# Adapter A placed beside W1's columns, W's product made three chunks ahead, the next x turned two chunks earlier: a two-layer kernel on one Trainium2 core

## The chip, the cores and the metric

The kernel runs on one core of a Trainium2 chip. The metric is the device time of one execution in microseconds, lower being better.

## The reference

For each of 8 batch entries, x is [256, 1024] and mask is [1024, 1024] of 0 and 1. Two residual layers follow one another:

```python
# first layer: W and b shared, one coefficient and one mask for each batch entry
y = x + einsum('bsi,oi->bso', x, W0) + b0 + coeff[b] * einsum('bsi,bio->bso', x, 2 * mask - 1)
# second layer: W1 and b1 shared, a rank-16 adapter chosen by itok_B_6_15 for each entry
A, Bw = lora_A_w[ids], lora_B_w[ids]
out = y + einsum('bsd,od->bso', y, W1) + b1 + einsum('bsr,bor->bso', einsum('bsd,brd->bsr', y, A), Bw)
```

The mask of each entry makes a weight matrix of its own: W0 + I + coeff * (2 * mask - 1), with 4 MB of int32 mask read for each.

## The kernel before

**Precision.** Every float32 operand of a product is split into two fp32r parts, hi and lo, and a product is made of three: hi with hi, hi with lo, lo with hi.

**Chunks.** The work is 64 chunks, n = 8 * b + c: batch entry b (called a batch below), and 128 of the 1024 columns of y (c). For chunk n:

- SyncE (`load_mask`, L166) loads 512 KB of mask into one of four slots of `wm`, once the chunk four before has left it (semaphore `w_lo`).
- VectorE `make_w` (L482) makes 2 * coeff * mask + W0 in place; ScalarE `chunk_hi` (L343) makes `whi`; VectorE `chunk_lo` (L491) makes `wlo`. `whi` and `wlo` have three slots (WS = 3).
- TensorE `layer1` (L614): for each of 8 blocks k, one matmul of 512 columns (`whi` by x hi and x lo side by side) and one of 256 (`wlo` by x hi), into PSUM bank 4 or 5.
- ScalarE `half_y` (L370), VectorE `make_y` (L499), ScalarE `y_parts_hi` (L379) and VectorE `y_parts_lo` (L504) turn the bank into `yhl`, y hi and y lo, in one of two slots.
- TensorE, one chunk later (m = n - 1): `adapter_h` (L632), one matmul of 512 columns with the adapter's A as weights, summed over the batch's 8 chunks in bank 6; and `layer2` (L640), for each half of the rows (st) and of the output columns (oh) three matmuls of 512 columns with y as weights and W1 moving, into banks 0 to 3.

**End of a batch.** After the eighth chunk, `h_parts_hi` (three ScalarE copies, L385) and `h_parts_lo` split the adapter's h into the rows of `ht`. `finish` (L657) adds h times adapter B and the bias b1 to the four banks, one matmul of 512 columns each; three of them stand before the last three matmuls of `layer2`. ScalarE and VectorE copy two banks each into `zst` (`move_z`), and SyncE stores them.

**Order.** Each engine runs its list in the order written. SyncE's list for program step n is: load the mask of chunk n + 4; and, where c = 0, wait for the four moves of the batch before, store the four pieces, and issue the six small copies of adapter B into `bt` (`load_bt`, L201). So the masks of chunks 8b + 5 and later stand behind the stores of batch b - 1 in SyncE's queue. At c = 2 it loads the next x (`load_x`, four transfers of 256 KB). VectorE's list for step n in batches 1 to 7 is:

```python
if n + 2 < NS:
    make_w(n + 2)
if c in (5, 7) and b + 1 < NB:
    rows_lo(b + 1, (c - 5) // 2)
if n + 2 < NS:
    chunk_lo(n + 2)
make_y(n)
if c == 0:
    h_parts_lo(b - 1)
y_parts_lo(n)
```

and after it, at c = 0, two moves, and at c = 4 and 6 `turn_rows` (L462), a 32x32 block transpose of half of the next x, whose split (`rows_hi`, `rows_lo`) follows at c = 5 and 7. Batch 0 also transposes W0, W1, A and B on TensorE (`turn_unit`).

## Time and profile before

| | us |
|---|---|
| median of 3 runs | 433.26 (432.2 to 433.63) |
| the profiled execution, its own time | 435.75 |
| its span, first to last instruction | 434.1 |
| TensorE matmul busy (2049 matmuls) | 409.7 |
| VectorE busy | 287.1 |
| ScalarE busy | 184.6 |
| GpSimd busy | 24.0 |

The mean granted clock of TensorE over the span is 0.978 of full speed. The chain that ended last is made of TensorE work for 88% of the span and of VectorE work for 6%. Durations of matmuls in the trace include their latency, so the distance from one start to the next tells what one costs.

### The profile page before, as it was taken

How to read it: one execution, taken by the hardware profiler on the slowest of the kernel's cores; microseconds unless marked ns; L12 is line 12 of the kernel's file. 1: busy time of each engine (PE TensorE's matmuls, PEld its weight loads, DVE VectorE, ACT ScalarE, POOL GpSimd, SP SyncE). 2: the span in 40 equal slices, each digit the busy share in tenths (PEclk: the TensorE clock that was granted, in tenths of full speed). 3: DMA queues.
4: the chain of work that ended last, by engine and by line, in shares of the span. 5: the costliest groups of instructions: out<-in, count | busy, mean ns of one | idle time of the engine just before them, and what ended most of it. 6: DMA issues, size and time to landing. Idle time of an engine off the chain costs nothing.

```text
span 434.1 us, 5456 instructions
## 1 busy us (share of the span) xinstructions
PE 409.7 (94%) x2049; PEld 342.3 (79%) x2049; DVE 287.1 (66%) x336; ACT 184.6 (43%) x288; POOL 24.0 (6%) x47
## 2 busy tenths in 40 slices
PE   3579998978999999999999999999999999999996
PEld 3568886757888888888888888888888888888884
DVE  0475658676688666776588767776678667866512
ACT  2264555454334533363343434444245433453312
POOL 4325401000000000000000000000000000000000
PEclk9788999899999999999999999999999999999999
DMA  6996796416943399309931595319921894237002
GB/s 224 253 333 195 207 211 179 86 48 151 249 125 94 108 193 222 97 1 233 237 100 50 131 240 150 98 74 209 236 64 36 196 241 120 61 110 169 2 0 97
DMA packets 90845, 63.28 MB, mean 146 GB/s; under 512 B 3515, under 2 KB 84419, under 8 KB 90820
## 3 DMA queue, kind: packets, MB, share of 16 engines
q1 hardware_dynamic: 89588, 59.28, 55.3%
q0 software_dynamic: 1232, 3.67, 2.7%
q8 instruction: 16, 0.26, 0.3%
q14 instruction: 9, 0.07, 0.1%
HBM read 51.39 MB, written 8.39 MB: 138 GB/s over the span
## 4 chain that ended last, share of the span: by engine, by line
PE 88%; DVE 6%; ACT 2%; DMA 2%; issue 1%; SPq 1%; ACTq 0%; DVEq 0%
PE ps L625 27%; PE ps L627 13%; PE ps L652 13%; PE ps L651 13%; PE ps L653 13%; PE ps L635 3%; PE ps L611 3%; PE ps L663 2%; DMA cs<-in_condB_coeff_dram 2%; DVE wm L488 1%; DVE wlo L495 1%; ACT whi L350 1%; DVE w1lo L460 1%; DVE xhl L471 1%; DVE xt L465 0%
## 5 line engine op out<-in xcount | busy, mean ns | idle before, releaser
L625 PE MATMUL ps<-xhl,whi 128*128 128x512 f32 x512 | 187.8, 405 | 2.0 <-DVE wlo L495 1.2
L627 PE MATMUL ps<-xhl,wlo 128*128 128x256 f32 x512 | 145.1, 283 | 0.0
L495 DVE SCALAR_TENSOR_TENSOR wlo<-wm,cs_minus,whi 128x1024 fp32r<-128x1024 f32 x64 | 83.0, 1296 | 53.2 <-ACT whi L350 52.8
L625 PEld LDWEIGHTS ps<-xhl,whi 128*128 128x128 f32 x512 | 97.7, 191 | 25.1 <-DVE wlo L495 1.5
L350 ACT ACTIVATE whi<-wm,cs_minus 128x1024 fp32r<-128x1024 f32 x64 | 73.7, 1151 | 81.7 <-DVE wm L488 80.5
L651 PE MATMUL ps<-w1hi,yhl 128*128 128x512 f32 x256 | 102.0, 398 | 0.0
L652 PE MATMUL ps<-w1lo,yhl 128*128 128x512 f32 x256 | 100.7, 394 | 0.0
L653 PE MATMUL ps<-w1hi,yhl 128*128 128x512 f32 x256 | 100.5, 393 | 0.0
L627 PEld LDWEIGHTS ps<-xhl,wlo 128*128 128x128 f32 x512 | 98.1, 192 | 2.5
L488 DVE SCALAR_TENSOR_TENSOR wm<-wm,cs_twice,w0t 128x1024 f32<-128x1024 int32 x64 | 81.8, 1278 | 11.7 <-ACT w0t L331 11.5
L652 PEld LDWEIGHTS ps<-w1lo,yhl 128*128 128x128 f32 x256 | 48.5, 189 | 10.7
L653 PEld LDWEIGHTS ps<-w1hi,yhl 128*128 128x128 f32 x256 | 48.2, 188 | 10.8
L651 PEld LDWEIGHTS ps<-w1hi,yhl 128*128 128x128 f32 x256 | 48.6, 190 | 7.9
L376 ACT ACTIVATE ysum<-ps,b0col 128x256 f32<-128x256 f32 x64 | 30.0, 469 | 41.2 <-PE ps L627 40.6
L383 ACT ACTIVATE yhl<-ysum 128x256 fp32r<-128x256 f32 x64 | 26.7, 417 | 44.1 <-DVE ysum L502 43.5
L506 DVE TENSOR_TENSOR yhl<-ysum,yhl 128x256 fp32r<-128x256 f32 x64 | 27.1, 424 | 24.0 <-ACT yhl L383 23.7
L502 DVE TENSOR_TENSOR ysum<-ps,ysum 128x256 f32<-128x256 f32 x64 | 26.8, 419 | 19.2 <-ACT ysum L376 19.2
L465 DVE STREAM_TRANSPOSE xt<-xraw 128x1024 f32<-128x1024 f32 x14 | 30.4, 2174 | 0.0
L361 ACT ACTIVATE xhl<-xt 128x1024 fp32r<-128x1024 f32 x14 | 14.9, 1062 | 31.1 <-DVE xt L465 31.1
L635 PE MATMUL ps<-yhl,at 128*128 128x512 f32 x64 | 25.9, 404 | 0.0
L460 DVE TENSOR_TENSOR w1lo<-ps,w1hi 128x512 fp32r<-128x512 f32 x16 | 10.9, 688 | 13.6 <-ACT w1hi L341 13.6
L331 ACT ACTIVATE w0t<-ps 128x512 f32<-128x512 f32 x16 | 9.5, 597 | 22.8 <-PE ps L611 22.8
(50 smaller groups left out, 178.7 us busy)
## 6 DMA issues: line engine op xcount, KB each, us to landing
wm<-in_mask_Bx4096x_ik_dram SPq DMA_DIRECT2D x64, 512.0 KB, 5.8
out_dram<-zst SPq DMA_DIRECT2D x32, 256.0 KB, 2.5
xraw<-in_x_dram SPq DMA_DIRECT2D x28, 256.0 KB, 7.4
w1raw<-_L_cond_base_weight_dram SPq DMA_DIRECT2D x8, 512.0 KB, 6.5
bt<-bhl SPq DMA_DIRECT2D x48, 64.0 KB, 2.9
w0raw<-in_L_cond_W_dram POOLq DMA_DIRECT2D x5, 512.0 KB, 6.7
w0raw<-in_L_cond_W_dram SPq DMA_DIRECT2D x3, 512.0 KB, 9.2
xrows<-in_x_dram SPq DMA_DIRECT2D x2, 512.0 KB, 7.0
```

Source lines behind the costliest of these rows:

```text
L350: nc.scalar.activation(whi[:, n % WS, :, :], wm[:, n % MS, :].rearrange("p (k o) -> p k o", k=KT), ACT.Identity, bias=cs_minus[:, b:b + 1] ...
L376: nc.scalar.activation(ysum[:, n % 2, :], ps[:, L1B + n % 2, S:2 * S], ACT.Identity, bias=b0col[:, n % KT:n % KT + 1]).then_inc(y_half, 1)
L465: nc.vector.transpose(xt[:, :, :].rearrange("p t (n q) -> p n t q", q=Q), xraw[:, :, :].rearrange("p n (i k) -> p n k i", k=KT)[:, :, g * ...
L488: nc.vector.scalar_tensor_tensor(chunk, chunk.bitcast(I32), cs_twice[:, b:b + 1], w0t[:, c, :, :].rearrange("p k o -> p (k o)"), ALU.mult, ...
L495: nc.vector.scalar_tensor_tensor(wlo[:, s, :, :], wm[:, n % MS, :].rearrange("p (k o) -> p k o", k=KT), cs_minus[:, b:b + 1], whi[:, s, :, ...
L506: nc.vector.tensor_tensor(yhl[:, n % 2, S:2 * S], ysum[:, n % 2, :], yhl[:, n % 2, 0:S].bitcast(F32), ALU.subtract).then_inc(y_lo, 1)
L625: nc.tensor.matmul(ps[:, bank, :], whi[:, s, k, :], xhl[:, b % 2, k, :], start=(k == 0), stop=False, skip_group_check=True)
L627: op = nc.tensor.matmul(ps[:, bank, 0:S], wlo[:, s, k, :], xhl[:, b % 2, k, 0:S], start=False, stop=(k == KT - 1), skip_group_check=True)
L635: op = nc.tensor.matmul(ps[:, HB, :], at[:, c, b * 2 * R:b * 2 * R + P], yhl[:, n % 2, :], start=(c == 0), stop=(c == KT - 1))
L651: nc.tensor.matmul(ps[:, Z0 + j, :], hi, w1hi[:, c, cols], start=(c == 0), stop=False)
L652: nc.tensor.matmul(ps[:, Z0 + j, :], hi, w1lo[:, c, cols], start=False, stop=False)
L653: op = nc.tensor.matmul(ps[:, Z0 + j, :], lo, w1hi[:, c, cols], start=False, stop=False)
```

## The change

- `w1hi` and `w1lo` get 16 free columns on either side of W1's 1024. From batch 1 on GpSimd copies the batch's adapter A (hi and lo) into them (`place_a`): left of W1 for even batches, right of it for odd ones. `adapter_h` stays for batch 0 alone. From batch 1 on `layer2` covers the 1040 columns of A and W1 in three groups of 352, 344 and 344 columns for each half of the rows, so 18 matmuls a chunk in place of 13, into banks 0, 2, 3 and 1, 6, 7.
- h now comes out with the rows of x on the partitions. At the batch's end ScalarE copies it out (`move_h`), TensorE turns it back with two transposes into a free bank (`turn_h`), and the split into `ht` takes two ScalarE copies instead of three. For this the groups with A (j = 0) of the last chunk are multiplied one program step earlier, ahead of the next batch's first `layer1`.
- All six `finish` matmuls stand at the end, one behind another. There are six moves and six stores (328 to 352 columns) in place of four of 512.
- VectorE's list for step n becomes `chunk_lo(n + 2)`, `make_w(n + 3)`, then `rows_lo` (c = 3 and 5), `make_y(n)`, ..., with `turn_rows` at c = 2 and 4. ScalarE makes `chunk_hi(n + 3)` after `y_parts_hi(n)`. The number of slots of `wm`, `whi` and `wlo` is unchanged, and so is SyncE's order of masks, stores and `load_bt`. `load_x(b + 2)` stands at c = 7 instead of `load_x(b + 1)` at c = 2.
- A memset of the adapter's padding goes away in batch 0.

```diff
+
+    WR = R + D + R
+    EDGES = (0, 352, 696, D + R)
+    ZB = ((0, 2, 3), (1, 6, 7))
+
...
+
+    def z_cut(b, j):
+
+
+        g = j if b % 2 == 0 else 2 - j
+        lo, hi = EDGES[g], EDGES[g + 1]
+        if b % 2 == 0:
+            skip = R if j == 0 else 0
+            return slice(lo, hi), slice(skip, hi - lo), slice(lo + skip - R, hi - R), slice(0, R)
+        end = hi - R if j == 0 else hi
+        return slice(R + lo, R + hi), slice(0, end - lo), slice(lo, end), slice(hi - lo - R, hi - lo)
...
         w0t = sb("w0t", [P, KT, KT, P])
-        w1hi = sb("w1hi", [P, KT, D], F32R)
-        w1lo = sb("w1lo", [P, KT, D], F32R)
+        w1hi = sb("w1hi", [P, KT, WR], F32R)
+        w1lo = sb("w1lo", [P, KT, WR], F32R)
...
-        zst = sb("zst", [P, 4, HALF])
+        zst = sb("zst", [P, ST, D])
...
-        at = sb("at", [P, KT, (NB + 3) * 2 * R], F32R)
+        at = sb("at", [P, KT, 2 * P], F32R)
+        h_row = sb("h_row", [P, ST, R])
...
-            def store_z(b, st, oh):
-                if oh == 0:
-                    sp.wait_ge(z_moved_act, 2 * b + st + 1)
+            def store_z(b, q):
+                st = q // 2 if b == 0 else q // 3
+                if q % 2 == 0:
+                    sp.wait_ge(z_moved_act, moves_before(b) + q // 2 + 1)
                 else:
-                    sp.wait_ge(z_moved_dve, 2 * b + st + 1)
-                j = 2 * st + oh
-                dst = out[b, st * P:(st + 1) * P, oh * HALF:(oh + 1) * HALF]
-                sp.dma_start(dst, zst[:, j, :]).then_inc(z_stored[j], 16)
+                    sp.wait_ge(z_moved_dve, moves_before(b) + q // 2 + 1)
+                cols = slice(q % 2 * HALF, (q % 2 + 1) * HALF) if b == 0 else z_cut(b, q % 3)[2]
+                sp.dma_start(out[b, st * P:(st + 1) * P, cols], zst[:, st, cols]).then_inc(z_stored[st], 16)
...
@@ -243,17 +280,17 @@
                 if n == 7:
                     load_bt(0)
                 if c == 0 and b > 0:
-                    for st in range(ST):
-                        for oh in range(2):
-                            store_z(b - 1, st, oh)
+                    for q in range(4 if b == 1 else 6):
+                        store_z(b - 1, q)
                     load_bt(b)
-                if c == 2 and b + 1 < NB:
-                    load_x(b + 1)
+                if n == 2:
+                    load_x(1)
+                if c == 7 and b + 2 < NB:
+                    load_x(b + 2)
+            for q in range(6):
+                store_z(NB - 1, q)
             for st in range(ST):
-                for oh in range(2):
-                    store_z(NB - 1, st, oh)
-            for j in range(4):
-                sp.wait_ge(z_stored[j], 16 * NB)
+                sp.wait_ge(z_stored[st], 16 * stores_before(NB))
...
+            def place_a(b):
+                if b == 1:
+                    pool.wait_ge(parts_lo, parted(number["a", 0, 1]))
+                elif b >= 3:
+                    pool.wait_ge(l2_done, KT * (b - 1))
+                slot = 0 if b % 2 == 0 else R + D
+                for part, row in enumerate((w1hi, w1lo)):
+                    nc.gpsimd.tensor_copy(row[:, :, slot:slot + R],
+                                          at[:, :, (2 * b + part) * R:(2 * b + part + 1) * R].bitcast(F32)).then_inc(a_placed, 1)
...
-            nc.gpsimd.memset(at[:, :, 2 * P:].bitcast(F32), 0.0).then_inc(consts_set, 1)
...
+            place_a(1)
+            place_a(2)
+            pool.wait_ge(z_done, sums_before(1))
+            nc.gpsimd.memset(ht[0:80, :].bitcast(F32), 0.0).then_inc(h_cleared, 1)
+            for b in range(3, NB):
+                place_a(b)
...
-                nc.scalar.activation(zst[:, 2 * st, :], ps[:, Z0 + 2 * st, :], ACT.Copy).then_inc(z_moved_act, 1)
+            def move_h(b):
+                act.wait_ge(h_done, b + 1)
+                if b >= 2:
+                    act.wait_ge(h_turned, b - 1)
+                cut = z_cut(b, 0)[3]
+                nc.scalar.activation(h_row[:, :, :], ps[:, ZB[0][0]:ZB[1][0] + 1, cut],
+                                     ACT.Copy).then_inc(h_moved, 1)
+
+            def h_parts_hi(b):
+                act.wait_ge(h_turned, b)
+                act.wait_ge(h_cleared, 1)
+                act.wait_ge(z_done, sums_before(b))
+                nc.scalar.activation(ht[0:R, :], ps[0:R, L1B + (KT * b + 9) % 2, 0:S], ACT.Copy).then_inc(h_hi, 1)
+                act.wait_ge(h_hi, h_hi_before(b) + 1)
+                nc.scalar.activation(ht[96:96 + R, :], ht[0:R, :].bitcast(F32), ACT.Copy).then_inc(h_hi, 1)
...
+
+            def move_z(b, q):
+                st, j = divmod(q, 3)
+                act.wait_ge(z_done, sums_before(b) + q + 1)
+                act.wait_ge(z_stored[st], 16 * stores_before(b))
+                _, cut, cols, _ = z_cut(b, j)
+                nc.scalar.activation(zst[:, st, cols], ps[:, ZB[st][j], cut], ACT.Copy).then_inc(z_moved_act, 1)
 
             copy_w0(0, 0)
             copy_w0(0, 1)
@@ -433,22 +504,30 @@
                 if n == 1:
                     act.wait_ge(b1_in, 16)
                     nc.scalar.activation(b1hi[:, :], b1raw[:, :], ACT.Copy).then_inc(bias_hi, 1)
+            chunk_hi(KT + 2)
             for n in range(KT, NS):
                 b, c = divmod(n, KT)
-                if c in (5, 7) and b + 1 < NB:
-                    rows_hi(b + 1, (c - 5) // 2)
-                if n + 2 < NS:
-                    chunk_hi(n + 2)
+                if c in (3, 5) and b + 1 < NB:
+                    rows_hi(b + 1, (c - 3) // 2)
                 half_y(n)
-                if c == 0:
+                if c == 0 and b == 1:
+                    first_h_parts_hi()
+                elif c == 0:
                     h_parts_hi(b - 1)
                 y_parts_hi(n)
-                if c == 0:
-                    move_z(b - 1, 0)
-                    move_z(b - 1, 1)
+                if n + 3 < NS:
+                    chunk_hi(n + 3)
+                if c == 0 and b == 1:
+                    first_move_z(0)
+                    first_move_z(1)
+                elif c == 0:
+                    for q in (0, 2, 4):
+                        move_z(b - 1, q)
+                if c == 7:
+                    move_h(b)
             h_parts_hi(NB - 1)
-            move_z(NB - 1, 0)
-            move_z(NB - 1, 1)
+            for q in (0, 2, 4):
...
-                nc.vector.tensor_copy(zst[:, 2 * st + 1, :], ps[:, Z0 + 2 * st + 1, :]).then_inc(z_moved_dve, 1)
+            def h_parts_lo(b):
+                dve.wait_ge(h_hi, h_hi_before(b) + 1)
+                nc.vector.tensor_tensor(ht[32:32 + R, :], ps[0:R, L1B + (KT * b + 9) % 2, 0:S], ht[0:R, :].bitcast(F32),
+                                        ALU.subtract).then_inc(h_lo, 1)
...
+
+            def move_z(b, q):
+                st, j = divmod(q, 3)
+                dve.wait_ge(z_done, sums_before(b) + q + 1)
+                dve.wait_ge(z_stored[st], 16 * stores_before(b))
+                _, cut, cols, _ = z_cut(b, j)
+                nc.vector.tensor_copy(zst[:, st, cols], ps[:, ZB[st][j], cut]).then_inc(z_moved_dve, 1)
 
             dve.wait_ge(coeff_in, 16)
             nc.vector.tensor_scalar(cs_twice[:, :], cs[:, :], 2.0, None, ALU.mult).then_inc(coeff_made, 1)
@@ -555,26 +644,32 @@
                     dve.wait_ge(bias_hi, 1)
                     nc.vector.tensor_tensor(b1lo[:, :], b1raw[:, :], b1hi[:, :].bitcast(F32),
                                             ALU.subtract).then_inc(bias_lo, 1)
+            make_w(KT + 2)
             for n in range(KT, NS):
                 b, c = divmod(n, KT)
                 if n + 2 < NS:
-                    make_w(n + 2)
-                if c in (5, 7) and b + 1 < NB:
-                    rows_lo(b + 1, (c - 5) // 2)
-                if n + 2 < NS:
                     chunk_lo(n + 2)
+                if n + 3 < NS:
+                    make_w(n + 3)
+                if c in (3, 5) and b + 1 < NB:
+                    rows_lo(b + 1, (c - 3) // 2)
                 make_y(n)
-                if c == 0:
+                if c == 0 and b == 1:
+                    first_h_parts_lo()
+                elif c == 0:
                     h_parts_lo(b - 1)
                 y_parts_lo(n)
-                if c == 0:
-                    move_z(b - 1, 0)
-                    move_z(b - 1, 1)
-                if c in (4, 6) and b + 1 < NB:
-                    turn_rows(b + 1, (c - 4) // 2)
+                if c == 0 and b == 1:
+                    first_move_z(0)
+                    first_move_z(1)
+                elif c == 0:
+                    for q in (1, 3, 5):
+                        move_z(b - 1, q)
+                if c in (2, 4) and b + 1 < NB:
+                    turn_rows(b + 1, (c - 2) // 2)
             h_parts_lo(NB - 1)
-            move_z(NB - 1, 0)
-            move_z(NB - 1, 1)
+            for q in (1, 3, 5):
+                move_z(NB - 1, q)
 
         @block.tensor
...
-            def finish(b, st, oh):
+            def layer2(n, st, j):
+                b, c = divmod(n, KT)
+                q = 3 * st + j
+                if c == 0 and q == 0:
+                    pe.wait_ge(a_placed, 2 * b)
+                if c == 0 and b == 1 and q == 0:
+                    pe.wait_ge(z_moved_act, 2)
+                    pe.wait_ge(z_moved_dve, 2)
+                elif c == 0 and b > 1 and q % 2 == 0:
+                    pe.wait_ge(z_moved_act, moves_before(b - 1) + q // 2 + 1)
+                elif c == 0 and b > 1:
+                    pe.wait_ge(z_moved_dve, moves_before(b - 1) + q // 2 + 1)
+                cols = z_cut(b, j)[0]
+                dst = ps[:, ZB[st][j], 0:cols.stop - cols.start]
+                hi = yhl[:, n % 2, st * P:(st + 1) * P]
+                lo = yhl[:, n % 2, S + st * P:S + (st + 1) * P]
+                nc.tensor.matmul(dst, hi, w1hi[:, c, cols], start=(c == 0), stop=False, skip_group_check=True)
+                nc.tensor.matmul(dst, hi, w1lo[:, c, cols], start=False, stop=False, skip_group_check=True)
+                op = nc.tensor.matmul(dst, lo, w1hi[:, c, cols], start=False, stop=(c == KT - 1), skip_group_check=True)
+                if q == 5:
+                    op.then_inc(l2_done, 1)
+                if c == KT - 1 and q == 3:
+                    op.then_inc(h_done, 1)
+
+            def turn_h(b):
+                pe.wait_ge(h_moved, b)
+                for st in range(ST):
+                    op = nc.tensor.transpose(ps[0:R, L1B + (KT * b + 9) % 2, st * P:(st + 1) * P], h_row[:, st, :], ident[:, :])
+                op.then_inc(h_turned, 1)
+
...
+
+            def finish(b, st, j):
+                if st == 0 and j == 0:
+                    pe.wait_ge(h_hi, h_hi_before(b + 1))
+                    pe.wait_ge(h_lo, b + 1)
+                    pe.wait_ge(bt_in, 96 * (b + 1))
+                _, cut, cols, _ = z_cut(b, j)
+                nc.tensor.matmul(ps[:, ZB[st][j], cut], ht[:, st * P:(st + 1) * P], bt[:, cols],
+                                 start=False, stop=True, skip_group_check=True).then_inc(z_done, 1)
 
...
+                    pe.wait_ge(consts_set, 2)
                     pe.wait_ge(w0_copied, copied(number["w0", 2, 1]))
                 if m < KT:
                     pe.wait_ge(parts_lo, parted(number["w1", m, 1]))
-                adapter_h(m)
-                layer2(m, 0, 0)
-                if 0 < n < KT:
-                    turn_unit("w1", n, 0)
-                layer2(m, 0, 1)
-                layer2(m, 1, 0)
-                if 0 < n < KT:
-                    turn_unit("w1", n, 1)
-                if m % KT == KT - 1:
-                    finish(m // KT, 0, 0)
-                    finish(m // KT, 0, 1)
-                    finish(m // KT, 1, 0)
-                layer2(m, 1, 1)
-                if m % KT == KT - 1:
-                    finish(m // KT, 1, 1)
-
+                if m < KT:
+                    adapter_h(m)
+                    first_layer2(m, 0, 0)
+                    if n < KT:
+                        turn_unit("w1", n, 0)
+                    first_layer2(m, 0, 1)
+                    first_layer2(m, 1, 0)
+                    if n < KT:
+                        turn_unit("w1", n, 1)
+                    if m == KT - 1:
+                        first_finish(0, 0)
+                        first_finish(0, 1)
+                        first_finish(1, 0)
+                    first_layer2(m, 1, 1)
+                    if m == KT - 1:
+                        first_finish(1, 1)
+                    continue
+                pe.wait_ge(y_lo, m + 1)
+                if m % KT < KT - 1:
+                    for st in range(ST):
+                        for j in range(3):
+                            layer2(m, st, j)
+                else:
+                    if n < NS:
+                        turn_h(m // KT)
+                    layer2(m, 0, 1)
+                    layer2(m, 1, 1)
+                    if n == NS:
+                        turn_h(m // KT)
+                    layer2(m, 0, 2)
+                    layer2(m, 1, 2)
+                    for st in range(ST):
+                        for j in range(3):
+                            finish(m // KT, st, j)
+                if n < NS and n % KT == KT - 1:
+                    pe.wait_ge(y_lo, n + 1)
+                    layer2(n, 0, 0)
```

## Rows read from the trace of the kernel before

**Rows 1.** The page: its head, and group rows of ScalarE and of the stores.

```profile
span 434.1 us, 5456 instructions
...
L350 ACT ACTIVATE whi<-wm,cs_minus 128x1024 fp32r<-128x1024 f32 x64 | 73.7, 1151 | 81.7 <-DVE wm L488 80.5
```

**Rows 2.** Busy time by stretch: batch 2, from its first sum to the next (PEclk 1.00 is full speed).

```profile
146.50:194.00 47.50, 47.50 (x238) 39.76 (x238) 34.38 (x40) 20.27 (x31) 0.00 (x0) 1.00 0.62 142
```

**Rows 3.** The chain that ended last: start, us; four transposes, and adapter_h two chunks apart.

```profile
37.14 0.44 PE ps L611 x4
...
151.07 0.24 PE ps L635
...
162.68 0.24 PE ps L635
```

**Rows 4.** Timeline, TensorE: adapter_h and the next layer-1 chunk (start, us, ...).

```profile
204.19 0.40 PE L635 MATMUL ps<-yhl,at 128*128 128x512 f32 x1
...
207.19 0.39 PE L625 MATMUL ps<-xhl,whi 128*128 128x512 f32 x1
```

**Rows 5.** Timeline, the last chunk: layer 1's end to both halves of y.

```profile
423.19 0.39 PE L635 MATMUL ps<-yhl,at 128*128 128x512 f32 x1
423.39 0.47 ACT L376 ACTIVATE ysum<-ps,b0col 128x256 f32<-128x256 f32 x1 [4.44 <-PE ps L627]
...
423.89 0.42 DVE L502 TENSOR_TENSOR ysum<-ps,ysum 128x256 f32<-128x256 f32 x1 [4.49 <-ACT ysum L376]
...
424.35 0.42 ACT L383 ACTIVATE yhl<-ysum 128x256 fp32r<-128x256 f32 x1 [0.49 <-DVE ysum L502]
...
424.80 0.43 DVE L506 TENSOR_TENSOR yhl<-ysum,yhl 128x256 fp32r<-128x256 f32 x1 [0.48 <-ACT yhl L383]
```

**Rows 6.** Timeline, VectorE alone, around a turn of x.

```profile
217.41 0.42 DVE L506 TENSOR_TENSOR yhl<-ysum,yhl 128x256 fp32r<-128x256 f32 x1 [0.48 <-ACT yhl L383]
217.75 2.19 DVE L465 STREAM_TRANSPOSE xt<-xraw 128x1024 f32<-128x1024 f32 x1
219.85 1.26 DVE L488 SCALAR_TENSOR_TENSOR wm<-wm,cs_twice,w0t 128x1024 f32<-128x1024 int32 x1
221.07 1.23 DVE L471 TENSOR_TENSOR xhl<-xt,xhl 128x1024 fp32r<-128x1024 f32 x1
```

**Rows 7.** Timeline, all engines, the end of batch 2 (SPq is SyncE's queue).

```profile
191.55 0.39 PE L635 MATMUL ps<-yhl,at 128*128 128x512 f32 x1
...
193.91 0.93 PE L663 MATMUL ps<-bt,ht 128*128 128x512 f32 x3
194.42 1.09 ACT L400 ACTIVATE zst<-ps 128x512 f32<-128x512 f32 x2 [0.60 <-PE ps L663]
...
195.04 1.83 SPq L218 DMA_DIRECT2D out_dram<-zst  x4
...
196.92 3.13 SPq L208 DMA_DIRECT2D bt<-bhl  x5
...
200.73 1.34 SPq L173 DMA_DIRECT2D wm<-in_mask_Bx4096x_ik_dram  x2
```

**Rows 8.** Time from issue to landing: all masks; the mask issued at 200.73; at 153.22.

```profile
DMA to landing us min/median/max: 3.8/5.8/12.6
...
wm<-in_mask_Bx4096x_ik_dram SPq DMA_DIRECT2D x1, 512.0 KB, 4.4
...
wm<-in_mask_Bx4096x_ik_dram SPq DMA_DIRECT2D x1, 512.0 KB, 5.5
```

**Rows 9.** Timeline, the end of batch 0: VectorE and the first sum.

```profile
98.39 0.41 DVE L511 TENSOR_TENSOR ht<-ps,ht 32x256 fp32r<-32x256 f32 x1
...
98.91 0.93 PE L663 MATMUL ps<-bt,ht 128*128 128x512 f32 x3 [1.78 <-ACT ht L394]
```

**Rows 10.** Timeline, the end of the last batch.

```profile
428.43 0.84 PE L663 MATMUL ps<-bt,ht 128*128 128x512 f32 x3
...
429.48 1.81 SPq L218 DMA_DIRECT2D out_dram<-zst  x4
```

More of the change, by code:

```diff
@@ L55, in x_split, with sums_before, moves_before, stores_before @@
         return 4 + 2 * (b - 1) + g + 1
+    def z_cut(b, j):
[6 more added lines that the diff above has]
+        return slice(R + lo, R + hi), slice(0, end - lo), slice(lo, end), slice(hi - lo - R, hi - lo)
+    def sums_before(b):
+        return 4 + 6 * (b - 1) if b else 0
+    def moves_before(b):
+        return 2 + 3 * (b - 1) if b else 0
+    def stores_before(b):
+        return 2 + 3 * (b - 1) if b else 0
+    def h_hi_before(b):
+        return 3 + 2 * (b - 1) if b else 0
     with ExitStack() as ctx:
@@ L116, in two_layer_kernel @@
         bt_in = sem("bt_in")
-        z_stored = [sem(f"z_stored{j}") for j in range(4)]
+        z_stored = [sem(f"z_stored{st}") for st in range(ST)]
         ident_set = sem("ident_set")
@@ L142, in two_layer_kernel @@
         l2_done = sem("l2_done")
+        a_placed = sem("a_placed")
         h_done = sem("h_done")
+        h_cleared = sem("h_cleared")
+        h_moved = sem("h_moved")
+        h_turned = sem("h_turned")
         h_hi = sem("h_hi")
@@ L156, in part_views @@
             if kind == "w1":
-                return (w1hi, w1lo)[part][:, c, h * HALF:(h + 1) * HALF], src
+                return (w1hi, w1lo)[part][:, c, R + h * HALF:R + (h + 1) * HALF], src
             if kind == "a":
-                dst = at[:, 4 * h:4 * h + 4, 0:2 * P].rearrange("p k (b two r) -> p k b two r", b=NB, two=2)
+                dst = at[:, 4 * h:4 * h + 4, :].rearrange("p k (b two r) -> p k b two r", b=NB, two=2)
                 return dst[:, :, :, part, :], src.rearrange("p (k b r) -> p k b r", k=4, b=NB)
@@ L383, in y_parts_hi, with first_h_parts_hi @@
                 nc.scalar.activation(yhl[:, n % 2, 0:S], ysum[:, n % 2, :], ACT.Copy).then_inc(y_hi, 1)
-            def h_parts_hi(b):
-                act.wait_ge(h_done, b + 1)
-                if b == 0:
-                    act.wait_ge(consts_set, 3)
-                else:
-                    act.wait_ge(z_done, 4 * b)
+            def first_h_parts_hi():
+                act.wait_ge(h_done, 1)
+                act.wait_ge(consts_set, 2)
                 nc.scalar.activation(ht[0:2 * R, :], ps[0:2 * R, HB, 0:S], ACT.Copy).then_inc(h_hi, 1)
@@ L638, in adapter_h, with first_layer2 @@
                     op.then_inc(h_done, 1)
-            def layer2(n, st, oh):
-                b, c = divmod(n, KT)
+            def first_layer2(c, st, oh):
                 j = 2 * st + oh
-                if c == 0 and b > 0:
-                    if oh == 0:
-                        pe.wait_ge(z_moved_act, 2 * (b - 1) + st + 1)
-                    else:
-                        pe.wait_ge(z_moved_dve, 2 * (b - 1) + st + 1)
-                hi = yhl[:, n % 2, st * P:(st + 1) * P]
-                lo = yhl[:, n % 2, S + st * P:S + (st + 1) * P]
-                cols = slice(oh * HALF, (oh + 1) * HALF)
+                hi = yhl[:, c % 2, st * P:(st + 1) * P]
+                lo = yhl[:, c % 2, S + st * P:S + (st + 1) * P]
+                cols = slice(R + oh * HALF, R + (oh + 1) * HALF)
                 nc.tensor.matmul(ps[:, Z0 + j, :], hi, w1hi[:, c, cols], start=(c == 0), stop=False)
```

32 lines of the change are left out of this document (16 added, 16 removed).

## The prediction

> **What bounds the kernel now.** I read the page first, for the span [rows 1]. The busy time by stretch then shows that a middle batch lasts 47.50 us and TensorE works in all of it at full clock [rows 2]; the other middle batches read alike. In the chain two adapter matmuls two chunks apart stand 11.61 us apart, so a chunk costs 5.80 us [rows 3]. Eight chunks are 46.42; the four finishing matmuls at 0.23 make 0.92; 0.17 is left, a short stall at the batch's end. So from batch 1 on the kernel is a queue of matmuls, and a chunk can only become shorter if TensorE has less to do and everything else still arrives in time. Batch 0 is ruled by transposes, splits and loads; the change hardly touches it except at its end.
>
> **What a matmul costs.** Layer 2 with the adapter is 13 matmuls of 512 columns in 3.00 us, and 2.99 on average (5.80 less layer 1) [rows 4]: 0.230 each. At 2.4 GHz 512 columns are 0.213, so some 0.016 comes on top. Layer 1 gets the other 2.81: eight pairs of 512 and 256 columns, 0.351 a pair against 0.320 for the columns, again 0.016 each. The width 344 isn't in the trace; it lies between 256 (0.122) and 512 (0.230), and by the same line it is 0.159, and 352 is 0.163. The new layer 2 is 6240 columns in 18 matmuls: 2.60 + 18 x 0.016 = 2.89, that is 0.10 less for a chunk, and a chunk costs 5.70. The bounds: no extra cost for the five more matmuls gives 0.18 less, an extra cost of 0.022 each gives nothing.
>
> The Trainium skill, TensorE: Matmul & The Clock Gate, section Back-to-back issue gap, gives a fixed 2.5 ns beside the columns. By that figure the new layer 2 would save 0.16 us a chunk, or 9.0 in all in place of 5.6; the trace disagrees, since 512 columns would then be 0.216 apart and are 0.230 [rows 4].
>
> **The sum on TensorE.** Layer 2: 56 chunks x 0.10 = 5.6 saved. Two transposes a batch, at 0.11 each [rows 3]: 7 x 0.22 = 1.5 added. Six finishing matmuls over the same columns in place of four: 7 x 0.03 = 0.2 added. The stall of 0.17 at six batch ends, if the new path of h is in time: 1.0 saved. Is it? Call T0 the end of layer 1 of a batch's first chunk. The transposes end near T0 + 0.45, ScalarE is then past half_y (T0 + 0.67 by the distances of [rows 5]), two copies of about 0.4 end at 1.5 and VectorE's part at about 1.55; the finish isn't wanted before 12 matmuls later, T0 + 2.1. Yes, with 0.5 to spare, so these edits are hidden. The GpSimd copies of A and the missing memset stand beside other work and are counted at nothing; uncovered, a copy would be some 1 us once a batch, but its columns aren't wanted for most of a batch.
>
> **The end of batch 0.** There VectorE is late and TensorE waits for h: h_parts_lo runs at 98.39 and the first finish at 98.91 after 1.78 idle [rows 9]. The new list puts make_w(11), 1.22 long [rows 6], ahead of make_y(8) and of this h. 1.2 us added.
>
> **The masks, where the gain goes.** make_w(n + 3) now stands in front of make_y(n) in VectorE's queue, but the mask loads are no earlier. The mask of chunk 8b + 5 is issued behind the stores and bt: at 200.73 where T0 is 191.55, so T0 + 9.2 [rows 7]. Before, it was used only in step 8b + 3. Now it is wanted in step 8b + 2, right after chunk_lo(8b + 4), near T0 + 10, which in itself puts it 4 us short. It is also issued later still: ScalarE does y_parts_hi (to 1.8), then chunk_hi of 1.15 [rows 1], and only then the first move, of about 0.5 (half of 1.09 for 512 columns is the upper bound [rows 7]); the stores start at T0 + 3.35. Six of them at 0.45 are 2.7, bt and what follows 3.8 (196.92 to 200.73): issue at T0 + 9.9. It lands 4.4 later, in one batch 5.5 [rows 8]; I take 4.5, so T0 + 14.4.
>
> Behind this make_w wait, in order on VectorE: make_y(8b + 2), y_parts_lo, turn_rows (new at c = 2), chunk_lo, make_w, rows_lo (new at c = 3), make_y(8b + 3), y_parts_lo. In starts from the landing: 0.06 wake, 1.22 make_w, 0.46 + 0.45 for y [rows 5], 0.34 to the turn, 2.10 turn, 1.22 make_w's like for chunk_lo, 1.22 make_w, 1.23 rows_lo [rows 6], 0.46 + 0.45 + 0.43 for y: 9.64, so T0 + 24.0. TensorE wants y of chunk 8b + 3 after layer 1 of 8b + 4. That is T0 + 5.90 (0.22 transposes, 1.92 for twelve matmuls, 0.95 finishing, 2.81 layer 1) + 3 x 5.70 = T0 + 23.0. It stands for 1.0 us. The y of 8b + 2 is just in time (T0 + 17.0 for 17.3). The second turn and split, at c = 4 and 5, let VectorE catch up nothing, as two steps take it 11.3 against 11.4 on TensorE, and it has caught up by c = 7 but for about 0.1. Batch 7 turns no x, so its lateness stays under the slack; batch 1 still has the four wide stores behind its sums and issues its mask some 2.8 after its second layer 1 (the others 4.0), and has none. So five batches, 2 to 6: 5 x 1.0 = 5.0 added.
>
> **The end.** Before, three finishing matmuls stand ahead of the last three of layer 2, and from 428.43 it is 5.6 to the end [rows 10]. Now all six stand behind: 0.7 later, a stall of 0.15 for h (its path is 1.33, six matmuls and two transposes between cover 1.17), and six stores at 0.45 in place of four, 0.7. Together 1.6 added.
>
> **Sum.** -5.6 + 1.5 + 0.2 - 1.0 + 1.2 + 5.0 + 1.6 = +2.9 on a span of 434.1. The profiled execution took 435.75 with what lies around its span; the median of the runs is 433.26, and the difference is added to that: 436.2.
>
> **Rivals.**
>
> *No lateness.* If the mask lands by T0 + 13.4, or VectorE's chain is 1 us shorter, TensorE never waits and the sum is -2.1: 431.2, faster. That is the other side, and its point is sharp: 1.0 us in a chain of 24. For it: landings vary, the shortest of the 64 takes 3.8 [rows 8], and x is no longer loaded right behind. Against it: three of the terms are exact distances of the trace, and the issue behind the stores can't be avoided. Chance 0.18.
>
> The Trainium skill, DMA: Bandwidth & Descriptors, section Anatomy of one DMA, fits 2.0 us plus bytes over 436 GB/s (measured for GpSimd's queue), an estimate of 3.2 us for 512 KB. By it the mask lands at T0 + 13.1 and this rival holds, 431.2; the trace has 4.4 and 5.5 for these transfers [rows 8], so it adds nothing to the chance.
>
> *Later masks.* At 5.5 to landing [rows 8] in every batch, y of 8b + 2 is late as well and each of five batches stands 2.1: 436.2 + 5.5 = 441.7. One batch of five shows it. Chance 0.12.
>
> *Something between:* landings at 4.0, or half of the batches, 432 to 434.5. Chance 0.17.
>
> *Narrow matmuls dearer:* if the fixed part is 0.022 or more at 344 columns, the 5.6 are gone. But then TensorE's steps are longer and VectorE's lateness shrinks by as much until c = 3, so only part shows: about 438. Chance 0.05.
>
> *The path of h late* by 0.5 at each batch end, for instance through the move queue on ScalarE: 7 x 0.5 = 3.5, 439.5. Against it the 0.5 to spare. Chance 0.05.
>
> The forecast: 0.43, with a range of its own of 434.7 to 438.
>
> **Range and chances.** A no-change would be within 0.3% (432.0 to 434.6), about what a measurement of this kernel can tell. The case without lateness, 431.2, is held at the low end and the case of later masks is cut at its upper part: 430.9 to 439.4. Faster: 0.18 and little else, 0.20. Same: the case between and the low tail of the forecast, 0.19. Slower: 0.61.
>
> **What the profile after would show.** Right: layer 2 as 18 matmuls 0.159 apart; make_w(8b + 5) idle in front for some 4 us, released by the mask's landing; TensorE idle about 1 us in front of layer 2 of chunk 8b + 3, released by VectorE's y_parts_lo, in batches 2 to 6; batches of 47.8; the first finish of batch 0 near 100.1. Wrong: middle batches of 46.8 with TensorE busy throughout (no lateness), or steps of 5.80 as before (narrow matmuls dearer), or waits in front of the finish. What would make it wrong most easily is the 1.0, a small difference between two sums of over 20 us.

## The result and the profile after

The changed kernel takes 439.88 us (439.2 to 441.95, 4 runs), the kernel before 433.44 in the same comparison: 1.46% slower, ratio 1.0146 (95% interval 1.0082 to 1.0209). The forecast was 436.2 with a range to 439.4: the direction is right, the size is more than twice what was forecast, and the time is outside the range. A second comparison, on another chip, gave 440.38 against 433.78, ratio 1.0135 (1.0102 to 1.0169).

The profiled execution of after spans 437.4, which looks like the forecast (434.1 + 2.9 = 437.0), but the two profiled executions are not alike in their granted clock: 0.978 before, 0.988 after. An execution of the changed kernel at 0.976 spans 439.0. That pair, +4.9, is the one to explain.

The page of after: the head, and the group of make_w (busy, mean ns of one, then idle before it and what ended most of that).

```profile
span 437.4 us, 6140 instructions
...
L567 DVE SCALAR_TENSOR_TENSOR wm<-wm,cs_twice,w0t 128x1024 f32<-128x1024 int32 x64 | 82.9, 1295 | 42.2 <-DMA wm<-in_mask_Bx4096x_ik_dram 32.0
```

VectorE waited for a mask for 32.0 us in all, where before there was one such wait of 0.25. The chain that ended last shows what that does; here it is in batch 3 (start, duration, engine and line).

```profile
196.99 0.79 PE ps L791 x5
197.78 0.93 DVE zst L607 x2
...
198.84 0.46 SPq L255
...
200.82 0.59 SPq L245
...
203.99 0.59 SPq L246
...
204.62 4.17 DMA wm<-in_mask_Bx4096x_ik_dram
208.82 1.28 DVE wm L567
210.10 0.34 DVE ysum L581
210.47 0.43 ACT yhl L436
...
211.26 2.24 DVE xt L544
213.50 1.17 DVE wlo L574
214.67 1.19 DVE wm L567
215.86 1.14 DVE xhl L550
217.00 0.34 DVE ysum L581
217.37 0.42 ACT yhl L436
217.81 0.44 DVE yhl L585
...
218.29 0.42 PE ps L762
```

It is a ring: the sums (L791), the moves, six stores (L255), six bt copies (L245, L246), the mask, then VectorE's list in its new order, and only then layer 2 on TensorE. Before, the chain stayed on TensorE through such a batch. TensorE's own timeline at both ends of the ring, with T0 = 194.72 at the transposes of h (L773):

```profile
194.72 0.38 PE L773 MATMUL ps<-ident,h_row 128*16 128x128 f32 x2
194.86 0.40 PE L762 MATMUL ps<-w1hi,yhl 128*128 128x344 f32 x1
195.10 0.32 PE L763 MATMUL ps<-w1lo,yhl 128*128 128x344 f32 x1
195.26 0.32 PE L764 MATMUL ps<-w1hi,yhl 128*128 128x344 f32 x1
...
218.29 0.42 PE L762 MATMUL ps<-w1hi,yhl 128*128 128x344 f32 x1 [0.64 <-DVE yhl L585]
```

The mask is issued at T0 + 9.9 and landed by T0 + 14.07 (208.79); y of chunk 8b + 3 is there at T0 + 23.5 (218.25). The matmuls of layer 2 stand 0.157 us apart at 344 columns and 0.161 at 352. The idle time printed is short of the whole stall, since it counts from the modelled end of the matmul before, not from where the next could have started.

### The profile page after: what moved, and what is told of

It is laid out like the page before. It is cut to its first block, busy times and chain, and to the rows that moved or that the text cites. A ratio compares the mean times of both kernels' runs of the same rounds, so it can differ in the third digit from the quotient of the medians.

```text
span 437.4 us, 6140 instructions
## 1 busy us (share of the span) xinstructions
PE 405.3 (93%) x2357; PEld 367.5 (84%) x2357; DVE 285.5 (65%) x343; ACT 177.1 (40%) x295; POOL 28.9 (7%) x61
## 4 chain that ended last, share of the span: by engine, by line
PE 62%; DVE 17%; SPq 7%; DMA 7%; ACT 3%; issue 2%; DVEq 0%; ACTq 0%
PE ps L720 18%; PE ps L762 9%; PE ps L764 9%; PE ps L722 9%; PE ps L763 9%; DMA wm<-in_mask_Bx4096x_ik_dram 5%; DVE wm L567 5%; SPq L245 3%; PE ps L706 3%; DVE xt L544 3%; DVE wlo L574 3%; SPq L255 3%; DVE xhl L550 2%; DMA cs<-in_condB_coeff_dram 2%; PE ps L791 1%
## 5 line engine op out<-in xcount | busy, mean ns | idle before, releaser
L762 PE MATMUL ps<-w1hi,yhl 128*128 128x344 f32 (+1 forms) x336 | 109.5, 326 | 5.4 <-DVE yhl L585 5.3
L567 DVE SCALAR_TENSOR_TENSOR wm<-wm,cs_twice,w0t 128x1024 f32<-128x1024 int32 x64 | 82.9, 1295 | 42.2 <-DMA wm<-in_mask_Bx4096x_ik_dram 32.0
L764 PE MATMUL ps<-w1hi,yhl 128*128 128x344 f32 (+1 forms) x336 | 107.7, 321 | 0.0
L763 PE MATMUL ps<-w1lo,yhl 128*128 128x344 f32 (+1 forms) x336 | 107.6, 320 | 0.0
L574 DVE SCALAR_TENSOR_TENSOR wlo<-wm,cs_minus,whi 128x1024 fp32r<-128x1024 f32 x64 | 81.9, 1280 | 23.7 <-ACT whi L403 23.7
L762 PEld LDWEIGHTS ps<-w1hi,yhl 128*128 128x128 f32 x336 | 63.1, 188 | 10.8 <-DVE yhl L585 8.5
L763 PEld LDWEIGHTS ps<-w1lo,yhl 128*128 128x128 f32 x336 | 63.2, 188 | 0.0
L764 PEld LDWEIGHTS ps<-w1hi,yhl 128*128 128x128 f32 x336 | 63.1, 188 | 0.0
L414 ACT ACTIVATE xhl<-xt 128x1024 fp32r<-128x1024 f32 x14 | 14.8, 1060 | 19.1 <-DVE xt L544 19.1
L706 PE MATMUL ps<-ident,w0raw 128*128 128x128 f32 x64 | 11.3, 312 | 7.2 <-POOL w0raw L301 5.3
```

The lines of the kernel that those rows point to most:

```text
L567: nc.vector.scalar_tensor_tensor(chunk, chunk.bitcast(I32), cs_twice[:, b:b + 1], w0t[:, c, :, :].rearrange("p k o -> p (k o)"), ALU.mult, ...
L574: nc.vector.scalar_tensor_tensor(wlo[:, s, :, :], wm[:, n % MS, :].rearrange("p (k o) -> p k o", k=KT), cs_minus[:, b:b + 1], whi[:, s, :, ...
L762: nc.tensor.matmul(dst, hi, w1hi[:, c, cols], start=(c == 0), stop=False, skip_group_check=True)
L763: nc.tensor.matmul(dst, hi, w1lo[:, c, cols], start=False, stop=False, skip_group_check=True)
L764: op = nc.tensor.matmul(dst, lo, w1hi[:, c, cols], start=False, stop=(c == KT - 1), skip_group_check=True)
```

## The experiments

Times are medians; the kernel before took 433.78 or 433.84 in the same comparisons. "Batch" is the distance from one batch's h_parts_lo to the next; in the kernel before it is 47.5 in all six.

**The changed kernel again** (no edit).

> The changed kernel as it is, for its spread and its distance to the kernel before on one chip. If the gap between the two profiled executions (437.4 against 434.1 of span) is the whole truth, the pair differs by about 3.3 us; if the profile of before was a slow one of its runs, by 6 to 7 us. The theory of the late mask has the middle batches at 47.3 to 49.1 us, with VectorE's make_w of chunk 8b + 5 released by the mask's landing in each; the rival (VectorE's list is too long in any case) has the same times but no need of that release.

440.38. Five middle batches (2 to 6) of 48.97, 47.48, 47.44, 47.88 and 48.86 us; in the first profile 49.06, 47.36, 47.34, 48.07 and 48.13. VectorE's make_w of chunk 8b + 5 is released by the mask's landing in each batch. The medians differ by 6.6; at like clock the two kernels differ by about 5 (section below).

**Masks ahead of the stores.**

```diff
-                if n + 4 < NS:
-                    load_mask(n + 4)
+                ahead = (n + 4, n + 5, n + 6) if b > 0 and c == 0 else () if b > 0 and c in (1, 2) else (n + 4,)
+                for u in ahead:
+                    if u < NS:
+                        load_mask(u)
```

> The changed kernel, with the masks of chunks 8b + 5 and 8b + 6 issued ahead of the stores of batch b - 1. Late mask theory: no waits of TensorE for VectorE in the middle batches, each 46.8 us (46.7 + little), 6.2 us less over batches 2 to 6, so a span of 431.2. Rival, VectorE's new list (turn and split in steps 3 to 6 ahead of make_y) is too long in any case: waits of about 1 us a batch stay, span about 436. Rival, narrow matmuls or the path of h: waits elsewhere stay, span about 437.

431.11, ratio to the kernel before 0.9927 (0.9897 to 0.9956): faster. Batches 2 to 6 are 46.35, 46.29, 46.35, 46.29 and 46.35, shorter than the 46.8 of the expectation: the narrower matmuls give more than I took. SyncE's queue in its profile, around the same batch end:

```profile
190.15 0.54 SPq L210 DMA_DIRECT2D wm<-in_mask_Bx4096x_ik_dram  x1
196.01 2.83 SPq L255 DMA_DIRECT2D out_dram<-zst  x6
198.88 3.13 SPq L245 DMA_DIRECT2D bt<-bhl  x5
```

The last of the three masks is out 6 us before the stores, and neither VectorE waits for a mask nor TensorE for VectorE from batch 1 on. VectorE's list is the same as in the changed kernel, so the rival "the list is too long in any case" is out, and so are dear narrow matmuls and a late h: one edit of SyncE's order takes 9 us away (440.38 to 431.11).

**The adapter part alone:** the old order on VectorE and ScalarE in the changed kernel, and the x load at c = 2 again. VectorE's side of the edit:

```diff
-                if n + 2 < NS:
-                    chunk_lo(n + 2)
-                if n + 3 < NS:
-                    make_w(n + 3)
-                if c in (3, 5) and b + 1 < NB:
-                    rows_lo(b + 1, (c - 3) // 2)
+                if n + 2 < NS:
+                    make_w(n + 2)
+                if c in (5, 7) and b + 1 < NB:
+                    rows_lo(b + 1, (c - 5) // 2)
+                if n + 2 < NS:
+                    chunk_lo(n + 2)
...
-                if c in (2, 4) and b + 1 < NB:
-                    turn_rows(b + 1, (c - 2) // 2)
+                if c in (4, 6) and b + 1 < NB:
+                    turn_rows(b + 1, (c - 4) // 2)
```

> The changed kernel with the old order on VectorE and ScalarE (product two chunks ahead, x turned at c = 4 and 6, x loaded at c = 2): the adapter part alone. Late mask theory: the mask of 8b + 5 is needed a step later and is in time (a wait of at most 0.7 us in VectorE that TensorE doesn't see). But y of the eighth chunk is wanted 2.9 us after its layer 1 and comes at 3.7, because a turn and a split stand ahead of it: 0.85 a batch in batches 1 to 6, middle batches of 47.6. Sum against before: -5.6 + 1.5 + 0.2 - 1.0 + 5.1 + 1.6 = +1.8, span about 435.9. If the late mask isn't what costs, this one is as slow as the changed kernel, 437.4.

438.1, ratio 1.0104 (1.0073 to 1.0135). One wait of TensorE a batch, in front of the early groups of the eighth chunk:

```profile
233.46 0.43 PE L758 MATMUL ps<-w1hi,yhl 128*128 128x344 f32 x1 [1.19 <-DVE yhl L582]
```

Three of the batches 2 to 6 last 47.76 to 47.80; the other two, 48.42 and 50.25, are those in which VectorE also waited for a mask, 1.6 and 1.9. The longest has something more. TensorE's wait in it is 2.10, and behind it the granted clock (the third figure from the end) is at its lower level from 379.1 to 382.6:

```profile
377.76 0.43 PE L758 MATMUL ps<-w1hi,yhl 128*128 128x352 f32 x1 [2.10 <-DVE yhl L582]
```

```profile
380.00:382.00 2.00, 2.00 (x8) 1.71 (x7) 1.28 (x1) 0.24 (x1) 0.00 (x0) 0.50 0.04 8
```

Of the 3.9 that this batch lies over 46.3, 1.6 to 1.8 is left when the wait is taken off. The waits of 1.19 and 1.79 in the other batches were not followed by a fall. The place of the wait is as forecast, its size larger: 1.45 over the 46.3 of a batch without waits, not 0.85. So the adapter part alone also loses, by another wait: it needs x out of the way of the eighth chunk.

**The order part alone:** the new order of VectorE, ScalarE and of the x loads in the kernel before (the reverse of the edit above, with chunk_hi(n + 3) behind y_parts_hi).

> The kernel before with the new order on VectorE and ScalarE and the new place of the x loads: the order part alone. Late mask theory: a chunk is still 5.80 and the first step 6.85, so TensorE wants y of 8b + 3 at T0 + 24.25, and VectorE has it at T0 + 9.7 + 4.5 + 9.6 = 23.8: no wait in most batches, 0 to 0.7 in one with a late landing; plus 1.2 at the end of batch 0, span 435.3 to 436. VectorE waits for the mask of 8b + 5 for some 4 us all the same. Rival, the new list is too long in any case: more than 1 us in each middle batch, span over 440.

436.88, ratio 1.0070 (1.0043 to 1.0097). VectorE waits for the mask of 8b + 5 in every batch, and TensorE has one short wait in batch 2 alone:

```profile
159.92 1.28 DVE L491 SCALAR_TENSOR_TENSOR wm<-wm,cs_twice,w0t 128x1024 f32<-128x1024 int32 x1 [4.62 <-DMA wm<-in_mask_Bx4096x_ik_dram]
...
169.38 0.49 PE L639 MATMUL ps<-yhl,at 128*128 128x512 f32 x1 [0.43 <-DVE yhl L509]
```

Batches 3 to 6 are 47.30 to 47.37, batch 2 is 48.07. So VectorE waits of 3.0 to 3.5 cost nothing where a chunk is 5.80: it is the adapter part, with its shorter chunks and later stores, that brings TensorE to the point where the wait shows. What this kernel loses lies in batch 2 and at the end of batch 0, where TensorE waits 2.96 and batch 1 takes 48.51.

**Chunk 11 made later:** the end of batch 0 alone.

```diff
-                if n + 3 < NS:
+                if KT < n < NS - 3:
                     make_w(n + 3)
...
                 y_parts_lo(n)
+                if n == KT:
+                    make_w(n + 3)
```

> The changed kernel with one edit: in step 8, VectorE makes W's chunk 11 behind y_parts_lo(8) instead of ahead of make_y(8), so that h of batch 0 is ready as before the change. Theory: the longer wait of TensorE at the end of batch 0 (2.9 us idle instead of 1.8) costs 1.0 us itself and another 1.4 because the granted clock falls to 1.2 GHz behind it. Then the wait is 1.8 again, the clock stays at 1.00 from 97 to 108 us, and 2.4 us are gained: about 437.5 median where the changed kernel had 440. Rival, the clock falls there for another cause: 1.0 us gained, clock at 0.5 as before.

439.25, not 437.5: the median hardly moves. The cause that was tried is confirmed all the same. In the changed kernel the end of batch 0 is this (VectorE's h_parts_lo; the first sums; then busy time by stretch, where the figure behind the five engines is the granted clock):

```profile
98.63 0.41 DVE L590 TENSOR_TENSOR ht<-ps,ht 32x256 fp32r<-32x256 f32 x1
...
99.14 1.24 PE L782 MATMUL ps<-bt,ht 128*128 128x512 f32 x3 [2.92 <-issue]
```

```profile
100.00:102.00 2.00, 2.00 (x6) 1.51 (x6) 0.69 (x1) 1.05 (x3) 0.00 (x0) 0.50 0.27 100
102.00:104.00 2.00, 2.00 (x10) 1.71 (x9) 1.87 (x3) 0.00 (x0) 0.31 (x1) 0.75 0.94 347
```

and with chunk 11 later it is this:

```profile
95.14 0.94 PE L784 MATMUL ps<-bt,ht 128*128 128x512 f32 x3 [1.72 <-ACT ht L444]
```

```profile
98.00:100.00 2.00, 2.00 (x14) 1.78 (x13) 2.00 (x2) 1.03 (x3) 0.00 (x0) 1.00 0.37 137
```

The wait is 1.72 again instead of 2.92, and the clock stays at its upper level, 2.4 GHz, instead of falling to 1.2, so the rival (another cause for the fall) is out. What was missed is the next thing in line: batch 1, which had been covered by its late and slow start, now runs into its own late mask (VectorE waits 5.98) and takes 49.33. That is 2.7 over the 46.64 of the next kernel, as much as the repair gives: 1.2 of wait and 1.5 of clock. The gain of one repair was handed to the other fault.

**Both repairs.**

> Both repairs: the masks of chunks 8b + 5 and 8b + 6 ahead of the stores, and chunk 11 made later. If the two causes are apart, it is the kernel with masks first (431.1 median) less 2.4: 428.7, middle batches of 46.35.

427.02, ratio 0.9850 (0.9811 to 0.9890). Batches: 46.64, then 46.35 and 46.29 in turn. Batch 1 was 48.14 with the masks first alone, so the fallen clock cost 1.50. The middle batches are as forecast, the median is not: it is 4.1 below 431.11, where 2.4 was expected. The fallen clock and the longer wait make at most 2.7 of it. The two medians come from different chips and from executions with different clocks in the opening; what the rest is isn't shown.

**Product two ahead, x in steps 3 to 6:** the old lookahead with the new place of x, masks behind the stores. VectorE's side of the edit (ScalarE's `chunk_hi` goes back to n + 2 as well):

```diff
-                if n + 2 < NS:
-                    chunk_lo(n + 2)
-                if n + 3 < NS:
-                    make_w(n + 3)
+                if n + 2 < NS:
+                    make_w(n + 2)
                 if c in (3, 5) and b + 1 < NB:
                     rows_lo(b + 1, (c - 3) // 2)
+                if n + 2 < NS:
+                    chunk_lo(n + 2)
```

> The changed kernel with the old order of W's product (make_w(n + 2) and chunk_hi(n + 2), two chunks ahead) but x still turned and split in steps 3 to 6, and the masks behind the stores. Late mask theory: the mask of 8b + 5 is wanted a step later, near T0 + 13.6, so VectorE waits for it little or not, y of 8b + 3 comes at about T0 + 20.7 for 22.8, and y of the eighth chunk is in time as no turn stands ahead of it: middle batches of 46.35 with no wait of TensorE, and the short wait at the end of batch 0 as before the change. Median about 428.7. Rival, turning x in steps 3 to 6 is what hurts: waits of 1 to 2 us a batch stay, about 438.

430.21, ratio 0.9895 (0.9863 to 0.9927). All middle batches are 46.76 or 46.77: no mask is late in them, and a wait of about 0.4, where none was forecast, is left at the eighth chunk:

```profile
232.73 0.43 PE L760 MATMUL ps<-w1hi,yhl 128*128 128x344 f32 x1 [0.19 <-DVE yhl L584]
```

So of the change's order the moved x is needed and does no harm, and the third chunk of lookahead is what made it slower.

**The kernel before with the masks first**, a control with the same edit of SyncE's queue.

> The kernel before with the masks of chunks 8b + 5 and 8b + 6 ahead of the stores, as a control: its VectorE waited for a mask once for 0.25 us in all, so late mask theory has no change, 433.8, within 0.3%. If it gets faster, masks cost something there too that the profile doesn't show.

434.33, ratio 1.0005 (0.9979 to 1.0030): no change. The edit is worth nothing where the mask isn't wanted early.

**Masks amid the bt copies:** chunk 11 later, and the masks behind the stores and three bt copies.

```diff
                 for r in range(0, 80, R):
+                    if b > 0 and r == 3 * R:
+                        for u in (KT * b + 5, KT * b + 6):
+                            load_mask(u)
                     sp.dma_start(bt[r:r + R, :].bitcast(F32), bhl[rows, 0, :].bitcast(F32)).then_inc(bt_in, 16)
...
-                if n + 4 < NS:
+                if n + 4 < NS and not (b > 0 and c in (1, 2)):
                     load_mask(n + 4)
...
```

> As the kernel with only chunk 11 made later (439.25 median), but the masks of 8b + 5 and 8b + 6 issued behind the six stores and three of the six bt copies: near T0 + 8.0 instead of 9.9, landing near T0 + 12.4. Late mask theory, with a threshold near T0 + 13.4: VectorE still waits some 2.4 us for the mask in each batch, y of 8b + 3 comes at T0 + 21.9 for 22.8, TensorE waits 0 (up to 0.3 where an issue takes 1 us longer), middle batches of 46.35 to 46.7, median about 427.5, as with the masks first. Rival, any wait of VectorE is passed on to TensorE in proportion: half of the stalls stay, about 433.

429.15, ratio 0.9873 (0.9837 to 0.9908), between the two forecasts and near the first. Its VectorE waits in batches 2 and 3:

```profile
155.06 1.28 DVE L570 SCALAR_TENSOR_TENSOR wm<-wm,cs_twice,w0t 128x1024 f32<-128x1024 int32 x1 [3.83 <-DMA wm<-in_mask_Bx4096x_ik_dram]
200.40 1.28 DVE L570 SCALAR_TENSOR_TENSOR wm<-wm,cs_twice,w0t 128x1024 f32<-128x1024 int32 x1 [2.27 <-DMA wm<-in_mask_Bx4096x_ik_dram]
```

The first makes a batch of 46.90, the second one of 46.30. (Batch 1, whose mask is later too, takes 47.25 in place of 46.64.) With this run the whole curve is there. For batches 2 to 6 of three profiles, when the mask of 8b + 5 had landed (start of make_w less 0.04, from T0, which is 1.16 before h_parts_lo) and how long the batch was:

| profile | landed after T0, us | batch, us |
|---|---|---|
| masks amid bt | 13.6, 12.0, 12.3, 12.4, 13.3 | 46.90, 46.30, 46.35, 46.29, 46.60 |
| changed kernel | 15.8, 14.05, 14.0, 14.8, 14.9 | 49.06, 47.36, 47.34, 48.07, 48.13 |
| changed kernel again | 15.7, 14.2, 14.2, 14.6, 15.6 | 48.97, 47.48, 47.44, 47.88, 48.86 |

Up to T0 + 13.0 a batch is 46.3; beyond it is 46.3 plus the whole lateness. "In proportion to VectorE's wait" is out: it is a threshold with a slope of one.

**The last stores on two queues:** both repairs, and in the last batch ScalarE issues three of the six stores behind its moves.

> Both repairs (427.0 median), and the last batch's six stores shared out: three on ScalarE's queue after its three moves, three on SyncE's. If the end is bound by SyncE's six issues at 0.45 one behind another, as forecast, the last sum to the end is 0.8 us shorter: 426.2. If it is bound by the last move and the landing, no change.

427.48, not told apart from 427.02. From the first sum to the end it is 6.2 in both profiles (421.61 to 427.8, 417.06 to 423.3). The issues are done earlier on SyncE, but the stores land 2.3 to 3.3 after issue instead of 1.9 to 2.1. Why they land later wasn't tried; in both profiles the DMA engines are 8 to 9 tenths busy for most of the stores' time, at 350 to 400 GB/s, so that moving the 1.05 MB may be what is left.

## Why the prediction was right and wrong

**Right: the mechanism and the sign.** The ring through stores, bt and mask, the place of the wait (chunk 8b + 3), the batches that have it (2 to 6), the issue at T0 + 9.9 (measured 9.9 in batch 3), VectorE's 9.64 from landing to y (measured 9.46): all as worked out, for a batch in which no issue is held up. In batches 3 and 4, which are such batches, the stall is 1.0 to 1.2 where 1.0 was forecast. That h would be in time was right too: no wait stands in front of the batches' sums, but for 0.16 in the last batch (0.15 forecast), and the end as a whole came out as forecast, 1.5 for 1.6. The copies of A that GpSimd makes, counted at nothing, take 0.29 each in the middle batches, and nothing waits for them.

One part was right by luck. Batch 1 was to have no stall, because its mask is issued sooner. It has none, but the kernel with only chunk 11 made later shows why: without the longer wait and the fallen clock at its start the same batch loses 2.7 to its late mask.

**Wrong: the terms of the sum.** For the pair at like clock (434.1 and 439.0), the forecast's +2.9 and the measured +4.9 split like this, the forecast's terms regrouped by stretch:

| term | forecast | measured |
|---|---|---|
| h of batch 0 later | +1.2 | +1.0 (98.91 to 99.89) |
| batches 2 to 6 without any stall | 5 x -0.72 | 5 x -1.18 (46.32 for 47.50) |
| late masks in them | +5.0 | +9.0 (240.63 less 5 x 46.32) |
| batch 1, batch 7 and the end | +0.3 | +0.8 (0.6 in batch 1, 48.13 for 47.50) |

The step that failed is the term "5 x 1.0" for the masks, a mis-sized one: it measured 9.0, or 1.8 a batch. Two things are in it, 0.4 each. I took one landing time, T0 + 14.4, for all batches; ten of them landed at 14.0 to 15.8, 14.8 on average. And the threshold is T0 + 13.0, not 13.4, because the shorter chunks (5.65, not 5.70) bring TensorE to the point sooner; what the shorter matmuls gave beyond the forecast, 2.3 over five batches, the late masks took back for the greater part. The landings are later by the issue alone: in the ten batches the mask is issued at T0 + 9.9 to 11.6, on average 10.6 where 9.9 was forecast, and lands 4.1 to 4.6 behind that, on average 4.2 where I took 4.5. SyncE's queue in after shows it:

```profile
148.89 3.81 SPq L255 DMA_DIRECT2D out_dram<-zst  x6
...
197.95 2.83 SPq L255 DMA_DIRECT2D out_dram<-zst  x6
```

At times a single issue takes 0.5 to 1.6 us longer than its like, in both profiles in batches 2, 5 and 6, and past the threshold every us in that queue is a us of the batch. The trace of before had such issues too, at the end of batch 6 for instance, where the four stores take 2.85 instead of 1.83:

```profile
385.00 2.85 SPq L218 DMA_DIRECT2D out_dram<-zst  x4
```

VectorE waited 0.25 for a mask behind it and TensorE not at all, and I left such issues out. They don't fall at random. Around the long store of batch 2 (149.77 to 151.23) the DMA view of after lists a transfer of 16 KB that no line of the kernel asks for, on a queue for instructions; from 197 to 206, where no issue is long, it lists none. From 149.7 to 151.3:

```profile
q1 hardware_dynamic: 274, 0.33, 57.1%
q8 instruction: 1, 0.02, 4.4%
```

Over all twelve profiles, from the end of batch 0 on, 35 issues of a store or a bt copy take more than 0.4 us longer than their like; at 33 of them such a transfer begins within 0.3 us of the start. That the one holds up the other is not shown: no run moved these transfers.

**Missed: the clock.** The forecast put the 1.2 at the end of batch 0 and went no further. The wait of TensorE grew from 1.8 [rows 9] to 2.9, the granted clock fell to half behind it, and that cost 1.5 more, a term that the sum doesn't have. In the table it is hidden in batch 1, where it is set against a gain of 0.9.

**Not in the sum at all:** the medians differ by 6.4 to 6.6, the pair at like clock by 4.9. In the opening of batch 0 both kernels have executions with a low granted clock and with a high one. Of the kernel before, the comparisons with the experiments hold 39 executions: nine at a mean clock of 0.978 to 0.980 span 433.2 to 435.1, the others (0.986 to 1.00) 430.2 to 433.0, but for one of 435.7. Of the changed one there are ten: six at 0.973 to 0.976 span 438.0 to 440.2, four at 0.985 to 0.994 span 436.6 to 438.3. At like clock they differ by about 5; the median of the changed kernel is one with the low clock, that of the kernel before is not. Whether the change itself makes the low clock more frequent stays open (the kernels with both repairs had it in two of six and one of six). The base of the forecast was such a case: the profiled execution of before has the low clock and lies 2.5 above the median, 433.26, to which its difference was added.

**The rivals.** "Later masks", 0.12, is what three of ten batches did (2.5 to 2.7 over 46.3). In them y of chunk 8b + 2 is late as well, as that rival has it: TensorE waits 1.10 for it at 164.10 in batch 2. The time ended between it and the forecast. "No lateness", 0.18, is what the masks put first make, and its 431.2 was met (431.11), but partly by luck: at a like low clock that kernel is 4.1 below before (430.0 and 434.1 of span) where the rival had 2.1, since the shorter chunks give more than was taken and the fallen clock, 1.5, isn't in it; the median is 2.7 below. "The path of h late" adds 3.5 to 436.2, which makes 439.7 and not 439.5; it did not come.

The extra cost of a matmul over its columns was taken as 0.016 at every width. It is 0.017 at 512 columns and 0.014 at 344 and 352, so the 18 narrow matmuls take 2.85, and a chunk costs 0.15 less than before instead of 0.10. The Trainium skill, TensorE: Matmul & The Clock Gate, section Back-to-back issue gap, which gives a fixed 2.5 ns for a matmul by itself, has neither cost right here, but the saving of 0.16 a chunk that was estimated from it came closer than mine. The Trainium skill, DMA: Bandwidth & Descriptors, section Anatomy of one DMA, led to an estimate of 3.2 us for a mask, by its fit for GpSimd's queue; on SyncE's queue the ten masks took 4.1 to 4.6.

## What to carry to other kernels

A longer lookahead of compute needs its loads to look ahead as far: before asking an engine to do something a step earlier, find the load's place in the issuing queue and what it stands behind, here six stores and six copies that can't start until the very engines that want the load have finished. In an in-order queue, work for the distant future must not stand ahead of work that is due now unless its input is certain; the wait costs nothing up to a threshold and everything beyond it, and making the bound engine faster moves the threshold towards you. And a change that is slower as a whole can hold a faster one: with the masks in front and one product moved, the same idea takes 427.0 instead of 433.8.

## What the runs showed of the hardware

- In eight profiles a wait of TensorE of 1.7 to 1.8 us at the end of batch 0 left the granted clock at 1.00; in the four where it was 2.9 us the clock fell to 0.5 (1.2 GHz) for 3.4 us of solid matmuls, 1.5 us lost behind a wait that was 1.2 longer. The adapter part alone has a wait of 1.79 without a fall behind it and one of 2.10 with.
- A matmul with its weight load costs 0.157 us at 344 columns and 0.230 at 512 at full clock, so 0.014 to 0.017 over its columns at 2.4 GHz; splitting 13 matmuls into 18 narrower ones is cheap as long as columns are saved.
- A DMA issue of SyncE, 0.45 for a store and 0.59 for a bt copy, now and then takes 0.5 to 2 us longer; at 33 of 35 such issues a 16 KB transfer on an instruction queue begins within 0.3 us of the start.
- Halving a queue's stores between two issuing engines saved issue time and lost as much in landing (2.3 to 3.3 us after issue instead of 1.9 to 2.1).
